# Vision tower on one core: output projections in the first three steps of the feed-forward loop, rare experts first, output bias added behind the features, class rows on another semaphore

## The chip, the cores and the metric

One of the eight cores of a Trainium2 chip runs the whole program. The metric is the device time in microseconds (us) of one execution; lower is better. All arithmetic is float32, but for a few one-hot products in bfloat16.

## What is computed

A small vision tower over 32 images. Each image becomes 25 patches, a class row is put in front, and so there are 32 x 26 = 832 rows of 256 numbers. Cut to what matters:

```python
h = patches @ W                                  # 768 -> 256, and the class row in front of each image
h = h + attn0(norm(h)) @ Wo.T + bo               # linear attention ACROSS images, per position; elu(q)+1, elu(k)+1
h = h + ffn0(norm(h))                            # fixed split of the rows over 8 experts:
                                                 #   x + norm(x) @ attn_w.T, gelu(x @ w1[e]), @ w2[e], @ next_w, gelu
h = h + attn1(norm(h))                           # causal linear attention in each image, 16 heads
x = norm(h); s = shared_down(silu(x@sg) * (x@su))        # 256 -> 512 -> 256 for every row
e = argmax(x @ gate_w); x = x * sigmoid(max(x @ gate_w)) # one of 32 routed experts for every row
h = h + s + down[e](silu(x @ gate[e]) * (x @ up[e]))     # 256 -> 512 -> 256, 1.5 MB of weights each
```

With the reference's own inputs 18 of the 32 routed experts get rows. Counted in strips of 32 rows they need: expert 0 three, 3 one, 4 six, 6 five, 8 one, 10 two, 27 two, and 11, 12, 13, 14, 15, 18, 19, 20, 24, 26, 29 one each; 31 strips in all. Among the first 104 rows (group 0) there are rows for 15 experts; four of them have fewer than four rows there: 8 (3 rows), 15 (2), 20 (1) and 26 (2). These are counts of the inputs, not times.

## The kernel before

The 832 rows lie in 8 groups of 104 (four images each). `h` holds them, rows on the partitions. Every stage runs over the groups, and `lagged(steps, stages)` (line 237) writes the order of a software pipeline: in step t it issues, for each `(stage, lag)` in the list, `stage(t - lag)`. The same list idea is written out once for each engine, so each engine has its own fixed order, and semaphores join them.

**Start.** SyncE (SP) issues all loads in one queue (lines 275 to 303). TensorE's `tok(g)` (line 376) makes the patch product of a group, VectorE (DVE) adds the class rows (line 1033), takes the moments, GpSimd (POOL) raises the variance to the power -1/2 (`power`, line 1439, 104x2 elements), DVE normalises, TensorE transposes (`trA`). The second half of `tok(0)` waits until both the second half of the patch weights and the class rows are there (line 383); the identity comes behind the second part of the patches (line 283).

**First attention.** `unit(n)` (line 402), n = 0 to 7, makes the query and key features in eight pieces; ScalarE (ACT) makes relu and exp (lines 809 and 811), DVE `feature_max` (line 1050) and `feature_sum` (line 1056), then TensorE makes the values in seven tiles (line 427), and DVE adds their bias in `v0_evac` (line 1045). Tiles 2 to 6 wait for the evacuation of an earlier one. DVE's order is `feature_sum(n-1)`, `feature_max(n)`, and at the end `v0_evac(0)`, `feature_sum(7)`, `v0_evac(1)` and on. POOL adds the output bias `bo` to the whole of `h` in one instruction (line 1445), as soon as the last group is normalised. Then come the attention products and `wo(g)` (line 459), the output projection of a group; DVE adds it to `h` in `h1_norms(g)` (line 1076).

**Feed-forward loop.** `wo(0)` to `wo(2)` run ahead; then TensorE's loop (line 570) has in step t: `tr1(t-1)` (transpose of the normalised group), `tr2(t-3)`, `nx(t-2)` (the `next_w` product), `xa(t-1)` (the `attn_w` product), `wo(t)` for t of 3 to 7, `up(t-1)` and, three groups behind, `qk1(t-3)` and `v1(t-3)` (projections of the second attention), `down(t-1)`. In the step of group g, ACT makes the eight gelus (line 848) between `up(g)` and `down(g)`; DVE's `xa_evac(g)` (line 1096) lies between `xa(g)` and `up(g)`, its `eo_evac(g)` (line 1103) between `down(g)` and `nx(g)`. `h1_norms(t)` has lag 0 on DVE.

**Second attention.** DVE and TensorE step through the groups; `first_look` (line 1220) reads the routing of group 0 while the rest is still computed, so that SP can load the weights of eight experts early (`early_at`, line 315): the first eight, by index, that group 0 uses. `seen` marks which experts group 0 uses, `seen_rank` is its running sum.

**Shared expert and routing tables.** TensorE makes `shared_up(n)` (line 637), DVE the products `hidden(n)` (line 1256), and between them DVE builds the tables (lines 1264 to 1326): which rows go to which slot, the order of the experts, where their weights lie. An expert's place in the order (its rank) is: the eight early ones by index, then all others by index (`chosen` has one row of 32 flags for each of these two kinds; the tables are running sums over both).

**Routed experts.** Four strips of 32 rows make a quad; the 31 strips are 8 quads, q = 0 to 7, of which TensorE computes gate and up (`strips`, line 698, for both the line 703), then transposes `hw` (`ht`, line 709) and makes the down product of the quad before (line 716). The weights of a quad are copied from one of eight slots (1.5 MB each) to fixed lanes, by DVE (`copy_gate`, `copy_up`, `copy_down`, lines 1334 to 1346) and ACT (line 920), one quad ahead. SP loads the other ten experts with `feed` (line 330), two in flight, n-th into the slot of the expert of rank n; a feed waits until the last quad that uses that slot's expert has been copied (lines 332, 333), and `loaded` is counted by SP in the same queue. While the routed quads run, TensorE also makes the shared down products of groups 2 to 7: by the list `SHARED_AT` one in q = 3, two in q = 4 and three in q = 5. The rows of `h` go out by a DMA of POOL (line 1467), and when all eight are stored, POOL adds the routed rows to the output, one indirect DMA for each quad (line 1460).

## Time and profile before

| | us |
|---|---|
| median of 3 runs | 328.4 |
| lowest and highest of them | 328.25, 331.58 |
| the profiled execution, its own time | 330.19 |
| span of its instructions | 328.3 |
| so, around the span | 1.89 |
| mean granted TensorE clock | 0.984 of full speed |

A profile shows one execution. TensorE's rows are PE (matrix products) and PEld (weight loads); a float32 product of 128x256 or so stands as two records. "Chain" is the chain of waits that ended last, in order of time; in the timeline a row's bracket says how long the engine was idle before it and what ended that. A granted clock of 1.00 is 2.4 GHz, one of 0.50 is 1.2 GHz.

### The profile page before, as it was taken

How to read it: one execution, taken by the hardware profiler on the slowest of the kernel's cores; microseconds unless marked ns; L12 is line 12 of the kernel's file. 1: busy time of each engine (PE TensorE's matmuls, PEld its weight loads, DVE VectorE, ACT ScalarE, POOL GpSimd, SP SyncE). 2: the span in 40 equal slices, each digit the busy share in tenths (PEclk: the TensorE clock that was granted, in tenths of full speed). 3: DMA queues.
4: the chain of work that ended last, by engine and by line, in shares of the span. 5: the costliest groups of instructions: out<-in, count | busy, mean ns of one | idle time of the engine just before them, and what ended most of it. 6: DMA issues, size and time to landing. Idle time of an engine off the chain costs nothing.

```text
span 328.3 us, 6678 instructions
## 1 busy us (share of the span) xinstructions
PE 296.7 (90%) x2495; PEld 213.1 (65%) x2495; DVE 197.9 (60%) x565; ACT 142.5 (43%) x320; POOL 58.4 (18%) x65
## 2 busy tenths in 40 slices
PE   7999969689899999999999898988998999998585
PEld 5776548588799999999887566654454334553131
DVE  0556972413364464554368999848872998727636
ACT  1113555322332242232554756529155876506533
POOL 0124300000010010100000010110741002111853
PEclk9999999879999999999999999999999999999899
DMA  7999998006255170000000000699955658999551
GB/s 255 410 436 417 421 347 216 0 0 216 76 224 184 74 257 2 0 2 0 3 0 3 2 2 2 258 426 431 419 181 186 285 186 310 342 384 388 77 60 21
DMA packets 12906, 61.57 MB, mean 188 GB/s; under 512 B 1562, under 2 KB 7530, under 8 KB 9290
## 3 DMA queue, kind: packets, MB, share of 16 engines
q1 hardware_dynamic: 10890, 58.25, 46.5%
q0 software_dynamic: 1984, 2.89, 4.5%
q8 instruction: 20, 0.33, 0.4%
q14 instruction: 12, 0.10, 0.1%
HBM read 55.09 MB, written 6.04 MB: 186 GB/s over the span
## 4 chain that ended last, share of the span: by engine, by line
PE 60%; DVE 19%; DMA 12%; issue 4%; ACT 3%; POOL 1%; SPq 1%; ACTq 0%; DVEq 0%; POOLq 0%
DMA arena<-experts_dram 10%; PE P L493 10%; PE P L505 9%; PE P L372 9%; PE P L703 5%; PE P L384 5%; PE P L645 4%; PE P L550 4%; DVE cols L1056 2%; PE P L716 2%; PE P L481 2%; PE P L588 2%; DMA arena<-cls_dram 2%; DVE arena L1050 1%; DVE arena L1103 1%
## 5 line engine op out<-in xcount | busy, mean ns | idle before, releaser
L1439 POOL TENSOR_TENSOR rstd<-var,mhalf 104x2 f32<-104x2 f32 x32 | 22.1, 692 | 190.3 <-DVE var L1013 150.5
L372 PE MATMUL P<-arena 128*104 128x256 f32 x192 | 48.4, 386 | 2.2 <-DVE arena L1103 0.8
L703 PE MATMUL P<-arena,cols 128*32 128x512 f32 x288 | 34.7, 622 | 6.3 <-ACT cols L945 5.3
L920 ACT ACTIVATE arena<-arena 128x1024 f32 x31 | 31.6, 1051 | 16.3 <-SPq L351 7.8
L372 PEld LDWEIGHTS P<-arena 128*104 128x104 f32 x192 | 30.1, 170 | 10.8 <-DVE arena L1103 3.0
L493 PE MATMUL P<-arena 128*128 128x104 f32 x256 | 32.7, 290 | 1.6 <-issue 1.0
L493 PEld LDWEIGHTS P<-arena 128*128 128x128 f32 x256 | 32.3, 206 | 2.5 <-issue 2.1
L505 PE MATMUL P<-arena 128*128 128x104 f32 x256 | 29.9, 275 | 2.4 <-ACT arena L848 2.4
L505 PEld LDWEIGHTS P<-arena 128*128 128x128 f32 x256 | 29.7, 192 | 3.1 <-issue 1.4
L848 ACT ACTIVATE arena<-P,arena 128x104 f32<-128x104 f32 x64 | 17.0, 348 | 28.9 <-PE P L493 28.9
L703 PEld LDWEIGHTS P<-arena,cols 128*32 128x32 f32 x288 | 8.7, 113 | 26.3 <-issue 16.8
L645 PE MATMUL P<-cols,arena 128*128 128x416 f32 x64 | 23.8, 520 | 1.8 <-DVE arena L1256 1.8
L833 ACT ACTIVATE arena<-P,arena 128x104 f32<-128x104 f32 x16 | 6.1, 433 | 40.9 <-PE P L472 40.9
L384 PE MATMUL P<-arena 128*104 128x256 f32 x96 | 22.6, 385 | 0.8 <-DMA arena<-cls_dram 0.8
L1103 DVE TENSOR_SCALAR arena<-P,arena 128x104 f32<-128x104 f32 x16 | 4.5, 321 | 25.9 <-PE P L505 25.9
L384 PEld LDWEIGHTS P<-arena 128*104 128x104 f32 x96 | 15.8, 173 | 5.8 <-DMA arena<-cls_dram 1.2
L645 PEld LDWEIGHTS P<-cols,arena 128*128 128x128 f32 x64 | 11.7, 190 | 10.9 <-issue 8.1
L716 PE MATMUL P<-arena,cols 128*32 128x256 f32 x192 | 15.4, 381 | 1.1 <-ACT cols L948 1.1
L550 PE MATMUL P<-arena 128*128 128x104 f32 x128 | 15.7, 275 | 0.0
L550 PEld LDWEIGHTS P<-arena 128*128 128x128 f32 x128 | 15.0, 192 | 0.2
L798 ACT ACTIVATE cols<-P 128x104 f32<-128x104 f32 x16 | 4.3, 366 | 24.2 <-PE P L394 24.2
L1019 DVE TENSOR_SCALAR arena<-h,mv,rstd 104x256 f32<-104x256 f32 x16 | 6.6, 414 | 13.0 <-POOL rstd L1439 13.0
(219 smaller groups left out, 516.5 us busy)
## 6 DMA issues: line engine op xcount, KB each, us to landing
arena<-experts_dram SPq DMA_DIRECT2D x18, 1536.0 KB, 9.6
arena<-experts_dram SPq DMA_DIRECT2D x8, 2048.0 KB, 12.8
sorted_x<-arena SPq DMA_DIRECT2D x1, 2184.5 KB, 38.4
arena<-shared_dram SPq DMA_DIRECT2D x1, 1536.0 KB, 32.7
arena<-patches_dram SPq DMA_DIRECT2D x2, 624.0 KB, 7.4
arena<-w_dram SPq DMA_DIRECT2D x1, 1024.0 KB, 10.5
out_dram<-arena SPq DMA_DIRECT2D x1, 1024.0 KB, 35.8
arena<-patches_dram SPq DMA_DIRECT2D x1, 936.0 KB, 7.8
```

Source lines behind the costliest of these rows:

```text
L372: last = mm(P[b][0:a.shape[1], col:col + D], a, rhs(c), start=(c == 0), stop=(c == chunks - 1))
L384: last = mm(P[g % 2][0:GT, 0:D], pat[:, g, c * GT:(c + 1) * GT], tokw_s[:, c, :], start=(c == 0), stop=(c == FC - 1))
L493: last = mm(bank(3 + m // 4, 4, GT)[:, m % 4, :], w[:, c, m * 128:(m + 1) * 128], xaT[:, c, :], start=(c == 0), stop=(c == DC - 1))
L505: last = mm(P[5][:, m * GT:(m + 1) * GT], w[:, c, m * 128:(m + 1) * 128], fhT[:, c, :], start=(c == 0), stop=(c == HC - 1))
L550: last = mm(bank(6, 4, GT)[:, 2 * w + m, :], w1_s[:, w, c, m * 128:(m + 1) * 128], x2T[:, c, :], start=(c == 0), stop=(c == DC - 1))
L645: last = mm(bank(b, HALF), w[:, c, m * 128:(m + 1) * 128], x3T[:, c, half * HALF:(half + 1) * HALF], start=(c == 0), stop=(c == DC - 1))
L703: last = mm(P[b][part, :], xT[:, c, part], weights(u)[:, c * INNER:(c + 1) * INNER], start=(c == 0), stop=(c == DC - 1), tile_position=(0, ...
L716: last = mm(P[3][part, 0:D], hT[:, c * 128 + STRIP * u:c * 128 + STRIP * (u + 1)], down_of(u, parity)[:, c * D:(c + 1) * D], start=(c == 0 ...
L848: A(fhT[:, m, :], bank(3 + m // 4, 4, GT)[:, m % 4, :], ACT.Gelu, bias=bcol_s[:, B1 + HC * g + m:B1 + HC * g + m + 1])\
L920: return A(to, third(where, n), ACT.Copy)
L1103: last = V.tensor_scalar(eoT[:, c, :], P[5][:, c * GT:(c + 1) * GT], bcol_s[:, B2 + DC * g + c:B2 + DC * g + c + 1], None, ALU.add)
L1439: nc.gpsimd.tensor_tensor(rstd[:, :], var[:, :], mhalf[:, :], ALU.pow).then_inc(s["rstd_ready"], 1)
```

## The change

Four things are changed at once. (1) All eight `wo` run in steps 0 to 2, four of them before the loop's first step, into banks 0, 7, 6 in turn. `xa` stands first in the step, `tr1(t)` just ahead of `down(t-1)`, and DVE normalises group t+1 in step t. (2) The experts that group 0 uses with fewer than four rows come first in the order, then its other experts, then the rest; the tables get three kinds, 96 columns in place of 64. (3) POOL's addition of `bo` waits for the eighth `feature_sum`. (4) The class rows and the identity count on one semaphore, and both are issued ahead of the second part of the patches; the second half of the patch weights has one of its own. The diff, cut:

```diff
+FEW = STRIP // GROUPS            # 4
+KINDS = 3 * EXPERTS              # 96
 def wo_bank(g):
-    return {1: 7, 2: 6}[g] if g in (1, 2) else 0
+    return (0, 7, 6)[g % 3]
 # SP
 if i == 0:
-    sp.dma_start(tokw_s[:, FC // 2:FC, :], tokw[:, FC // 2:FC, :]).then_inc(s["cls_in"], 16)
-    sp.dma_start(clsbuf, cls).then_inc(s["cls_in"], 16)
-if i == 1:
+    sp.dma_start(tokw_s[:, FC // 2:FC, :], tokw[:, FC // 2:FC, :]).then_inc(s["tokw2_in"], 16)
+    sp.dma_start(clsbuf, cls).then_inc(s["ident_in"], 16)
     sp.dma_start(ident[:, :], ident_in).then_inc(s["ident_in"], 16)
 # TensorE
 if g == 0 and c == FC // 2:
-    pe.wait_ge(s["cls_in"], 32)
+    pe.wait_ge(s["tokw2_in"], 16)
 def wo(g):
     if g >= 3:
-        pe.wait_ge(s["x2T_ready"], g - 2)
-        pe.wait_ge(s["h0_ready"], GROUPS + (g if g > 3 else 1))
+        pe.wait_ge(s["h0_ready"], GROUPS + g - 2)
...
-for g in range(3):
+for g in range(4):
     wo(g)
+tr1(0)
+wo(4)
 pe.wait_ge(s["wx_in"], 16)
+xa(0)
+wo(5)
...
+def last_wo(g):
+    if g in (1, 2):
+        wo(g + 5)
-lagged(GROUPS + 3, [(tr1, 1), (tr2, 3), (nx, 2), (xa, 1), (later_wo, 0), (up, 1), (but_last(qk1), 3), (but_last(v1), 3), (down, 1)])
+lagged(GROUPS + 3, [(but_first(xa), 1), (tr2, 3), (nx, 2), (up, 1), (but_last(qk1), 3), (but_last(v1), 3), (but_first(tr1), 0), (last_wo, 0), (down, 1)])
 # VectorE
-dve.wait_ge(s["cls_in"], 32)
+dve.wait_ge(s["ident_in"], 32)
...
 def h1_norms(g):     # h1_add(g), the addition of wo(g) to h, is a function of its own now
...
+    if g < 3:
+        h1_add((1, 3, 4)[g])
     dve.wait_ge(s["rstd_ready"], norms[0])
...
+    if g == 0:
+        h1_add(2)
+    if g == 2:
+        h1_add(5)
+h1_add(0)
+h1_norms(0)
-lagged(GROUPS + 2, [(nx_evac, 2), (xa_evac, 1), (h2_norm, 2), (h1_norms, 0), (but_last(z_evac), 3), (but_last(v_evac), 3), (attention_front, 1),
-                    (eo_evac, 1), (h2_bias, 2)])
+lagged(GROUPS + 2, [(xa_evac, 1), (nx_evac, 2), (h2_norm, 2), (h1_norms, -1), (but_last(z_evac), 3), (but_last(v_evac), 3), (attention_front, 1),
+                    (last_adds, 0), (eo_evac, 1), (h2_bias, 2)])
...
 if g == LOOK + 1:
-    V.tensor_scalar(seen, P[5][:, 256:256 + EXPERTS], 0.0, None, ALU.is_gt)
+    V.tensor_scalar(seen[:, EXPERTS:], P[5][:, 256:256 + EXPERTS], float(FEW), None, ALU.is_ge)
+    V.tensor_scalar(seen[:, 0:EXPERTS], P[5][:, 256:256 + EXPERTS], 0.0, None, ALU.is_gt).then_inc(s["seen"], 1)
...
-    link(V.tensor_tensor_scan(seen_rank, seen, zeros64[:, 0:EXPERTS], 0.0, ALU.add, ALU.add))
-    link(V.tensor_scalar(scratch32, seen_rank, at_k, None, ALU.is_le))
-    link(V.tensor_reduce(own[:, 0:1], scratch32, AX.X, ALU.add))
-    V.tensor_scalar_min(tcol[:, 2:3], own[:, 0:1], float(EXPERTS - 1)).then_inc(s["look"], 1)
+    dve.wait_ge(s["seen"], 1)
+    link(V.tensor_tensor(seen[:, 0:EXPERTS], seen[:, 0:EXPERTS], seen[:, EXPERTS:], ALU.subtract))
+    link(V.tensor_tensor_scan(seen_rank, seen, zeros[:, 0:2 * EXPERTS], 0.0, ALU.add, ALU.add))
+    link(V.tensor_scalar(seen_below, seen_rank, at_k, None, ALU.is_le))
+    link(V.tensor_reduce(own[:, 0:1], seen_below, AX.X, ALU.add))
+    link(V.tensor_scalar_min(own[:, 0:1], own[:, 0:1], float(2 * EXPERTS - 1)))
+    link(V.tensor_scalar(own[:, 1:2], own[:, 0:1], float(EXPERTS), float(-EXPERTS), ALU.is_ge, ALU.mult))
+    V.tensor_tensor(tcol[:, 2:3], own[:, 0:1], own[:, 1:2], ALU.add).then_inc(s["look"], 1)
...
-link(V.tensor_tensor(first_of, scratch64[:, 0:EXPERTS], scratch64[:, EXPERTS:], ALU.add))
+link(V.tensor_reduce(first_of, scratch.rearrange("p (a e) -> p e a", a=3), AX.X, ALU.add))
 # POOL
 pool.wait_ge(s["n_ready"], GROUPS)
+pool.wait_ge(s["qk0_ready"], 8)
 nc.gpsimd.tensor_tensor(h[:, :, :], h[:, :, :], brow_s[0:GT, BO0, :]...to_broadcast([GT, GROUPS, D]), ALU.add)
```

The waits of `tr2`, `qk1(0)` and `v1(0)` on the additions to `h` are set to the new order (`v1(0)` waits for all eight, since bank 7 takes `wo(1)`, `wo(4)` and `wo(7)`). The other table instructions have the same form over 96 columns.

## Rows read from the trace of the kernel before

**Rows 1.** The page's chain that ended last, shares by engine.

```profile
PE 60%; DVE 19%; DMA 12%; issue 4%; ACT 3%; POOL 1%; SPq 1%; ACTq 0%; DVEq 0%; POOLq 0%
```

**Rows 2.** Timeline, TensorE's first wait: start us, us, engine, line, operation.

```profile
7.51 4.20 PE L384 MATMUL P<-arena 128*104 128x256 f32 x18 [0.76 <-DMA arena<-cls_dram]
```

**Rows 3.** Timeline, the bias addition on POOL, DVE beside it, TensorE behind.

```profile
31.55 4.53 POOL L1445 TENSOR_TENSOR h<-h,arena 104x2048 f32<-104x2048 f32 x1 [0.59 <-DVE arena L1019]
32.07 4.45 DVE L1056 TENSOR_TENSOR cols<-arena 128x416 f32<-128x416 f32 x1
...
37.19 0.59 DVE L1056 TENSOR_TENSOR cols<-arena 128x416 f32<-128x416 f32 x1
...
45.03 4.73 PE L372 MATMUL P<-arena,cols 128*128 128x256 f32 x20 [2.81 <-DVE vrow L1045]
```

**Rows 4.** Timeline, DVE additions of PSUM and SBUF with POOL idle, then busy.

```profile
180.41 1.09 DVE L1195 TENSOR_TENSOR arena<-P,arena 104x416 f32<-104x416 f32 x2 [0.83 <-PE P L588]
...
189.73 0.69 POOL L1439 TENSOR_TENSOR rstd<-var,mhalf 104x2 f32<-104x2 f32 x1 [4.34 <-DVE var L1013]
...
190.14 1.09 DVE L1195 TENSOR_TENSOR arena<-P,arena 104x416 f32<-104x416 f32 x2
```

**Rows 5.** Windows: stretch, length, busy us of PE PEld DVE ACT POOL, clock, DMA.

```profile
42.00:44.00 2.00, 0.21 (x1) 0.00 (x0) 1.79 (x5) 1.87 (x4) 0.00 (x0) 1.00 0.94 380
...
64.00:66.00 2.00, 1.44 (x7) 1.28 (x7) 1.53 (x6) 0.56 (x1) 0.06 (x1) 0.50 0.00 0
```

**Rows 6.** Timeline, the first transpose of the loop, behind `wo(2)`.

```profile
61.43 0.55 PE L472 MATMUL P<-ident,arena 104*128 104x104 f32 x4 [1.36 <-DVE arena L1089]
```

**Rows 7.** The chain in order of time, the loop's first two steps.

```profile
64.75 6.52 PE P L493 x32
...
72.41 3.83 PE P L505 x32
...
84.41 3.80 PE P L505 x32
```

**Rows 8.** The chain, one later step, the next one's start, and the last step's gap.

```profile
101.49 0.57 DVE arena L1103 x2
...
104.08 0.86 PE P L372 x4
104.95 3.55 PE P L493 x32
...
114.74 0.57 DVE arena L1103 x2
...
157.10 0.52 issue
```

**Rows 9.** Timeline, DVE's running sums over 32 and 64 columns.

```profile
200.33 0.16 DVE L1227 TENSOR_TENSOR_SCAN arena<-arena 128x32 f32<-128x32 f32 x1
...
226.61 0.29 DVE L1271 TENSOR_TENSOR_SCAN arena<-arena 128x64 f32<-128x64 f32 x1
```

**Rows 10.** Timeline, TensorE's wait behind the tables.

```profile
229.51 3.06 PE L645 MATMUL P<-cols,arena 128*128 128x416 f32 x8 [1.58 <-DVE arena L1256]
```

**Rows 11.** Timeline of SP's queue, all ten feeds in one row.

```profile
250.75 46.27 SPq L334 DMA_DIRECT2D arena<-experts_dram  x10
```

**Rows 12.** The chain, first and last of four feeds in a row.

```profile
271.55 7.30 DMA arena<-experts_dram
...
296.68 9.87 DMA arena<-experts_dram
```

**Rows 13.** Timeline, gate and up products of quads 6 and 7.

```profile
298.85 3.64 PE L703 MATMUL P<-arena,cols 128*32 128x512 f32 x32 [1.09 <-ACT cols L945]
...
309.02 5.34 PE L703 MATMUL P<-arena,cols 128*32 128x512 f32 x32 [3.70 <-ACT cols L945]
```

**Rows 14.** Timeline, POOL's row additions, the first and the third.

```profile
302.98 1.71 POOL L1460 DMA_INDIRECT out_dram<-vrow,target x1 [6.37 <-DMA out_dram<-h]
...
306.90 2.01 POOL L1460 DMA_INDIRECT out_dram<-vrow,target x1 [0.30 <-issue]
```

More of the change, by code:

```diff
@@ L176, in tower @@
         slot_i = sb("slot_i", [GT, GROUPS], I32)
-        ranks = flat7[:, 0:640].rearrange("p (a e) -> p a e", a=10)
-        chosen, visits, load, ends, scratch64, zeros64 = (ranks[:, i, :] for i in range(6))
-        strips_of, raw = ranks[:, 6, 0:EXPERTS], ranks[:, 6, EXPERTS:]
-        others, seen = ranks[:, 7, 0:EXPERTS], ranks[:, 7, EXPERTS:]
-        seen_rank, scratch32 = ranks[:, 8, 0:EXPERTS], ranks[:, 8, EXPERTS:]
-        first_lg, first_max = ranks[0:GT, 9, 0:EXPERTS], ranks[0:GT, 9, EXPERTS:EXPERTS + 1]
-        first_of = scratch32
+        ranks = flat7[:, 0:10 * KINDS].rearrange("p (a e) -> p a e", a=10)
+        chosen, visits, load, ends, scratch, zeros = (ranks[:, i, :] for i in range(6))
+        strips_of, raw, others = (ranks[:, 6, i * EXPERTS:(i + 1) * EXPERTS] for i in range(3))
+        scratch32, first_of = ranks[:, 7, 0:EXPERTS], ranks[:, 7, EXPERTS:2 * EXPERTS]
+        first_lg, first_max = ranks[0:GT, 8, 0:EXPERTS], ranks[0:GT, 8, EXPERTS:EXPERTS + 1]
+        seen, seen_rank, seen_below = chosen[:, 0:2 * EXPERTS], visits[:, 0:2 * EXPERTS], scratch[:, 0:2 * EXPERTS]
         early_at = sb("early_at", [1, EARLY], I32)
@@ L656, in _ @@
             v1(GROUPS - 1)
-            def but_first(stage):
-                return lambda g: g > 0 and stage(g)
             lagged(GROUPS + 4, [(av, 1), (logits, 4), (tr3, 3), (but_first(den), 0), (but_first(scores), 0), (wo1, 1), (spread, 0), (shared_first, 2)])
@@ L1262, in _ @@
             rank, first, slot = (lgm[:, i * GROUPS:(i + 1) * GROUPS] for i in (3, 4, 5))
-            two = "p (a e) -> p a e"
+            kinds = "p (a e) -> p a e"
             V.tensor_scalar(raw, P[5][:, 256:256 + EXPERTS], 1.0 / STRIP, (STRIP - 1) / (2.0 * STRIP), ALU.mult, ALU.add)
-            V.scalar_tensor_tensor(chosen[:, EXPERTS:], P[5][:, 256:256 + EXPERTS], 0.0, others, ALU.is_gt, ALU.mult)
+            V.scalar_tensor_tensor(chosen[:, 2 * EXPERTS:], P[5][:, 256:256 + EXPERTS], 0.0, others, ALU.is_gt, ALU.mult)
             link(V.tensor_tensor(big[:, :, :], P[4][0:GT, 0:256].rearrange("p (g e) -> p g e", e=EXPERTS), onehot_b[:, :, :], ALU.mult))
@@ L1305, in _ @@
             some, rounds = tfl[:, 0:FEEDS], tfl[:, FEEDS:FEEDS + 1]
-            link(V.tensor_scalar(some, bcol_s[0:1, C_FEED:C_FEED + FEEDS], visits[0:1, EXPERTS - 1:EXPERTS], None, ALU.add))
-            link(V.tensor_scalar(some, some, visits[0:1, 2 * EXPERTS - 1:2 * EXPERTS], None, ALU.is_lt))
+            link(V.tensor_scalar(some, bcol_s[0:1, C_FEED:C_FEED + FEEDS], hits[0:1, :], None, ALU.add))
+            link(V.tensor_scalar(some, some, total[0:1, :], None, ALU.is_lt))
             link(V.tensor_reduce(rounds, some, AX.X, ALU.add))
             V.tensor_scalar(table[:, T_FEEDS:T_FEEDS + 1], rounds, 1.0, None, ALU.max)
-            link(V.scalar_tensor_tensor(scratch64, ends, at_k, chosen, ALU.is_le, ALU.mult))
+            link(V.scalar_tensor_tensor(scratch, ends, at_k, chosen, ALU.is_le, ALU.mult))
             V.tensor_scalar_add(own[:, 1:2], total, -1.0)
@@ L1314, in _ @@
             hidden(3)
-            link(V.tensor_reduce(own[:, 0:1], scratch64, AX.X, ALU.add))
+            link(V.tensor_reduce(own[:, 0:1], scratch, AX.X, ALU.add))
             link(V.tensor_scalar(own[:, 0:1], own[:, 0:1], own[:, 1:2], None, ALU.min))
@@ L1321, in _ @@
             all_quads, loops = tfl[:, FEEDS + 1:FEEDS + 1 + MAX_QUADS], tfl[:, FEEDS + 1 + MAX_QUADS:]
[L1322 removed]
+            link(V.tensor_scalar(all_quads, bcol_s[0:1, C_QUAD:C_QUAD + MAX_QUADS], ends[0:1, KINDS - 1:KINDS], None, ALU.is_lt))
             link(V.tensor_reduce(loops, all_quads, AX.X, ALU.add))
```

54 lines of the change are left out of this document (29 added, 25 removed).

## The prediction

> **What bounds the kernel now.** I read the page's chain first, then the chain in order of time, then the timeline where the chain changes its engine, and the windows for the clock. The chain lies 60% on TensorE, 19% on DVE and 12% on DMAs [rows 1]: TensorE is the bound, with a few stretches where something else is. They are these.
>
> Features, 31 to 45 us: POOL adds the output bias for 4.53 us. A `feature_sum` that DVE begins half a microsecond later takes 4.45 us; the same operation takes 0.59 us with POOL idle [rows 3]. From there DVE is late until the values, where TensorE stands still for 2.81 us [rows 3].
>
> Start of the loop, 57 to 88 us: TensorE waits for the first normalisation (1.36 us ahead of `tr1`) [rows 6], runs at half clock from about 64 us [rows 5], so that `up(0)` takes 6.52 us where a later `up` takes 3.55 [rows 7, 8], and waits for the last gelus (71.27 to 72.41, 1.14 us) [rows 7].
>
> Steady loop: one step is 114.74 - 101.49 = 13.25 us, 0.86 of it `wo` [rows 8], and the rest nearly all products. The last full step has a gap of 0.52 us where no `wo` is left between `xa` and `up` [rows 8].
>
> Routed experts, 250 us on: the ten feeds are issued from 250.75 to about 297 us, though nothing but their slots holds them back [rows 11], and at the end the chain is four feeds one behind the other, 7.30 to 9.87 us each, until 306.55 [rows 12]. But that chain overstates what they cost: TensorE meanwhile has the shared down products, and its real waits are 1.09 us ahead of quad 6 and 3.70 ahead of quad 7 [rows 13]. Behind the longer one the gate and up products take 5.34 us in place of 3.64 [rows 13].
>
> **The change, part by part.** All terms are for the profiled execution: 328.3 us of span and 1.89 around it, 330.19; the median of the runs is 1.8 lower, 328.4. I take the sum from either.
>
> *Class rows.* `tok(0)` waited 0.76 us for the class rows, the last of two transfers of one semaphore [rows 2]. They are the smallest thing in the queue there; without them I estimate 0.2 us less, and the identity, now ahead of the second patches, takes about as much back for `tok(1)`. Between -0.2 and 0.76 us; value 0.2.
>
> *Bias addition.* `feature_sum(0)` ends 3.9 us earlier (4.45 - 0.59) [rows 3]. What is late next is TensorE itself: units and two value tiles fill it until 42.2, and that is where its wait of 2.81 us began [rows 3], so the gain is 2.8 and not 3.9. POOL now adds from about 42.8 to 47.3 us, and its result is wanted only when the first `wo` is added to `h`, ahead of the normalisation that `tr1(0)` at 61.43 - 2.8 = 58.6 waits for [rows 6]: some eight microseconds of cover. Nothing else is queued on POOL before that. Beside it DVE has `v0_evac` and the mask products, one operand in PSUM and one in SBUF. Such additions take 1.09 us for two whether POOL is idle or begins 0.41 us before them [rows 4], while the operation that was held has both operands in SBUF [rows 3]. So I take no hold; the other end is the rest of the addition, 4.5 us.
>
> *Start of the loop.* `wo(3)` comes right behind `wo(2)`; `wo(4)` fits between `tr1(0)` and `xa(0)`, `wo(5)` between `xa(0)` and `up(0)`. These were waits, so `up(0)` begins as before against what lies ahead, and DVE's extra additions (0.42 us each or less) fall into the wait for POOL's power or behind the normalisation; `xa_evac(0)` now queues behind the normalisation of group 1 and is ready at about the same time. TensorE has then hardly half a microsecond of rest after 60 us, where it had 1.36 us and more before it fell to 1.2 GHz [rows 5, 6]. It kept 2.4 GHz through its 2.81 us wait at 42 us [rows 3, 5], so I expect the clock to stay: `up(0)` takes some 3.7 and not 6.52 [rows 7, 8]: gain 2.8. Neither end is shown: 0 if it falls anyway.
> Steps 1 and 2: the gelu waits (1.14 us each) [rows 7] now hold `tr1` (0.55) [rows 6] and `wo(6)`, `wo(7)` (0.86) [rows 8]; `xa` covers the wait for `eoT`. From the start of `down(0)` to that of `down(1)` it was 84.41 - 72.41 = 12.00 us [rows 7]; now `down` 3.8 [rows 7], `nx` and `xa` 2.0 without their wait (102.06 to 104.08), `up` 3.55 [rows 8], `tr1` and `wo` 1.4, less what overlaps at each seam: some 10.5. Gain 1.5.
>
> *Steady steps.* In five steps (t = 3 to 7) `wo` goes, 0.86 us [rows 8], and with `xa` and `tr2` (a microsecond together) between `down` and `nx`, DVE's 0.57 us of `eo_evac` [rows 8] is covered for good; today two transposes cover all but about 0.1 of it. So 1.0 a step, 5.0 together. What `wo` hid, DVE's `xa_evac` between `xa` and `up`, is now hidden by `tr2` and `nx`. It queues on DVE behind `eo_evac` and `h2_bias`; I estimate it ready 1.5 us after `down` ends, from three operations of 0.4 to 0.6, while `up` starts 2.1 to 2.3 after it. ACT's evacuation of `tr1` runs beside `down`, which lasts over 3.5 us. In t = 8 the gap of 0.52 goes [rows 8], the 0.1 too, and `tr1` has left this step: 1.2 less. Bounds: 0.3 a step if most of it comes back as waits, 1.1 at most.
>
> *Look and tables.* DVE is the bound through the second attention (the chain and the timeline show it nearly without a gap from 175 to 213 us). The look chain gets three more linked operations, and four of them work on 64 columns where it was 32: a running sum goes from 0.16 to 0.29 [rows 9]; the three short ones I put at 0.25 each with their wait, and a second comparison at 0.1, as short operations on DVE lie between the two sums of these rows: +1.1 us. In the tables the operations on 96 columns for 64 add, by the same rise of 0.13 us for 32 columns of a running sum and less for the others, 0.3 us ahead of `hidden(1)`, for which TensorE waited 1.58 us already [rows 10], and 0.3 later on: +0.6. Together 1.7 lost, between 0.8 and 2.3.
>
> *Rare experts first.* The order was 0, 3, 4, 6, 8, 10, 12, 13; it becomes 8, 15, 20, 26, 0, 3, 4, 6. In the first order the early eight hold 20 strips, and their slots come free after quads 0, 0, 2, 3, 3, 4, 4, 4; in the new one after quads 0, 0, 0, 0, 1, 1, 3, 4. The number of quads stays 8. (Both lists follow from the strips of each expert and `feed`'s waits.) Pairs of feeds take 7.3 to 9.9 us [rows 12]. At some 8.7 us a pair, feeds 0 and 1 go at 250.75 [rows 11] as now, 2 and 3 at about 260, 4 and 5 at 268.5, 6 at 277 and 7 behind it, landed at 286.5. The last pair waits for quad 5's copy, about 288 (today's third feed of the chain is issued then), and lands at 297. Quad 6 needs feeds 4 to 7 copied while quad 5 runs (from about 290), quad 7 the last pair from about 301: both are there. So 1.09 + 3.70 us of waiting go, and with them the 1.2 GHz behind the second [rows 13], 5.34 - 3.64 = 1.70: 6.5 us. What is late next is TensorE itself: from quad 6 to quad 7 it was 10.17 us, less 3.70 of waiting 6.47 [rows 13], and DVE and ACT copy a quad's weights beside it. Bounds: 0 if the feeds are not what quads 6 and 7 wait for, 6.5 above.
> Quad 0 now needs four early loads and not two, but they are asked for 33 us before it is copied.
>
> Sum: 0.2 + 2.8 + 2.8 + 1.5 + 5.0 + 1.2 + 6.5 - 1.7 = 18.3 us. 330.19 - 18.3 = 311.9 for the profiled execution, 328.4 - 18.3 = 310.1, say **310.0 us** for the median.
>
> **The rivals.**
> *POOL's row additions take the end over.* They start when the eight stores have landed, 302.98, and follow at 1.96 us ((306.90 - 302.98) / 2) [rows 14]. With the quads 6.5 us earlier the eighth is wanted by 316. If the stores land no sooner, the eighth is issued at 302.98 + 7 x 1.96 + 0.5 for the wait between = 317.2, and with additions slowed by denser copies (below) 2 us later: the tail gives 4 us and not 6.5: 312.5. For it: the stores are 0.1 MB each and cross the same feeds. Against: the last feeds now end 9 us earlier. DVE's copies beside an addition make it 2.01 us and not 1.71 [rows 14], so denser copies cost 0.3 each, 2 us more at worst.
> The Trainium skill, SBUF — State Buffer, SBUF: two separate sides, says more: copies of DVE from SBUF to SBUF lock out the writing of descriptors for POOL's DMAs, about 620 ns alone against 3100. By that each of seven additions beside copies would cost 2.5 us more, an estimate of 17 us that would eat the whole gain. The rows with and without copies differ by 0.3 us, so the trace does not bear this out at that size; I give it 0.01 of what is unnamed below.
>
> *The clock falls at the loop's start all the same:* 2.8 us less gain, 312.8. For it, that TensorE waits in three places there today; against, that the new products fill them.
>
> *The hold moves on to the values.* If POOL's addition holds `v0_evac` as it held `feature_sum`, TensorE waits some 4.5 us in the value tiles: the 2.8 turn into a loss of 1.7, 314.5. Against it stand rows 4.
>
> *The order of experts changes nothing* (the look sees other counts, or quads 6 and 7 wait for something else): 310.0 + 6.5 = 316.5.
>
> *The other side: slower.* The new step is a ring of waits: `tr1(t)` just ahead of `down`, ACT behind the gelus, `xa`, DVE's `xa_evac` behind `eo_evac` and `h2_bias` and DVE's normalisation of the next group ahead of the evacuations of `qk1` and `v1`, with POOL's power in it. If one of these isn't beside products but behind them, each of the eight steps pays it. The slack on `up` is 0.6 us. The change is slower only from 18.3 / 8 = 2.3 us of new wait a step. What stands in series at the loop's start today, from `tr1` to `up` (61.43 to 64.75, 3.3 us) [rows 6, 7], is the price where it lies open in each step: 310.0 + 8 x 3.3 = 336.
>
> **How the numbers follow.** The forecast 0.62; row additions 0.12; clock 0.07; hold 0.07; order without effect 0.06; ring of waits 0.03, and 0.03 for something unnamed that leaves it near the old time. A measurement of this kernel tells about 1% from no change, 3.3 us. All cases but the last two are faster by over 1%: 0.95; same 0.03, slower 0.02. The range reaches up over the first three rivals, and two of them together, to 316; down to 306, where the waits that go at the loop's start bring a little more than their terms, and the bounds of the tables and class rows are at their best.
>
> **What would show it.** `feature_sum(0)` at 0.6 us and no long DVE row beside POOL's 4.5 us; no wait of TensorE in the values; granted clock 1.00 from 60 to 72 us, `up(0)` under 4; steps of 12.2 to 12.3 us between the evacuations of line 1103's kind; feeds issued from 251 to 288 and none on the chain; the gate products of quads 6 and 7 at 3.64 us each without a wait before them. The prediction is wrong if steps stay above 12.8, if feeds stay on the chain, or if the last rows are POOL's additions in one unbroken run.

## The result, and the profile after

| us | before | after |
|---|---|---|
| median, lowest, highest (4 runs each, taken side by side) | 329.69, 328.25, 331.58 | 311.12, 310.22, 312.54 |
| the profiled execution, its span | 330.19, 328.3 | 310.22, 308.3 |
| mean granted clock of the profiled execution | 0.984 | 0.999 |

The ratio of the times is 0.944, 95% interval 0.937 to 0.951. The forecast was 310.0 us, 306 to 316: 18.4 us under the 328.4 it started from. Measured are 18.6 us under the 329.69 of the runs beside it.

The start of the profiled execution, timeline of TensorE, after:

```profile
6.95 1.54 PE L384 MATMUL P<-arena 128*104 128x256 f32 x6 [0.34 <-DMA arena<-tokw_dram]
8.93 2.84 PE L384 MATMUL P<-arena 128*104 128x256 f32 x12 [0.43 <-DMA arena<-patches_dram]
...
39.96 6.61 PE L372 MATMUL P<-arena,cols 128*128 128x256 f32 x28
...
58.16 0.58 PE L471 MATMUL P<-ident,arena 104*128 104x104 f32 x4 [0.41 <-DVE arena L1098]
...
61.50 3.71 PE L492 MATMUL P<-arena 128*128 128x104 f32 x32
```

The wait for the class rows [rows 2] is gone; shorter ones for weights and patches stand in its place. The values are one row of 28 records with no wait in it, where there were 2.81 us [rows 3]. The first transpose waits 0.41 us and not 1.36 [rows 6], and `up(0)` takes 3.71 us and not 6.52 [rows 7]. Beside the values, DVE and POOL, same view:

```profile
31.76 0.59 DVE L1061 TENSOR_TENSOR cols<-arena 128x416 f32<-128x416 f32 x1
...
42.45 4.53 POOL L1470 TENSOR_TENSOR h<-h,arena 104x2048 f32<-104x2048 f32 x1 [11.80 <-DVE cols L1061]
...
43.01 0.43 DVE L1050 TENSOR_TENSOR vrow<-P,arena 128x256 f32<-128x256 f32 x1 [0.39 <-PE P L372]
```

`feature_sum(0)` is at 0.59 us, and the `v0_evac` beside POOL's addition takes 0.43: no hold. The two windows of [rows 5] after (columns as there):

```profile
42.00:44.00 2.00, 2.00 (x10) 1.71 (x11) 1.17 (x4) 1.16 (x1) 1.54 (x1) 1.00 0.94 381
...
64.00:66.00 2.00, 2.00 (x18) 1.91 (x18) 0.00 (x0) 1.27 (x7) 0.00 (x0) 1.00 0.00 0
```

The chain in order of time, the loop's start and one later step, after:

```profile
61.66 3.55 PE P L492 x32
...
66.44 3.75 PE P L504 x32
...
76.75 3.79 PE P L504 x32
...
101.11 3.57 PE P L504 x32
...
113.19 3.57 PE P L504 x32
```

A step is 12.08 us (113.19 - 101.11) for 13.25 [rows 8], and between its rows nothing but TensorE stands. The look on DVE and what follows it on TensorE, timelines after:

```profile
185.46 0.13 DVE L1248 TENSOR_TENSOR arena<-arena 128x32 f32<-128x32 f32 x1
185.62 0.29 DVE L1249 TENSOR_TENSOR_SCAN arena<-arena 128x64 f32<-128x64 f32 x1
...
186.87 0.16 DVE L1254 TENSOR_TENSOR tcol<-own 128x1 f32<-128x1 f32 x1
```

```profile
188.09 0.92 PE L610 MATMUL P<-arena 104*32 104x104 f32 x32 [0.95 <-DVE arena L1215]
```

Before, TensorE's row of this kind came 0.1 us behind the one ahead of it (202.24 behind 202.11); now it waits for the addition that stands behind `first_look` on DVE. ("The look" below is this part of DVE's work.) The routed stage after: SP's feeds, the gate products of quads 6 and 7, POOL's stores and row additions (timelines):

```profile
237.05 39.42 SPq L334 DMA_DIRECT2D arena<-experts_dram  x10
```

```profile
283.99 3.64 PE L708 MATMUL P<-arena,cols 128*32 128x512 f32 x32
...
290.38 3.64 PE L708 MATMUL P<-arena,cols 128*32 128x512 f32 x32
```

```profile
278.91 0.55 POOL L1492 DMA_DIRECT2D out_dram<-h  x1 [7.17 <-DVE h L1374]
...
282.37 2.83 POOL L1492 DMA_DIRECT2D out_dram<-h  x1 [1.18 <-DVE h L1374]
287.46 1.74 POOL L1485 DMA_INDIRECT out_dram<-vrow,target  x1 [2.26 <-DMA out_dram<-h]
...
299.79 1.64 POOL L1485 DMA_INDIRECT out_dram<-vrow,target  x1 [0.30 <-issue]
...
301.74 1.72 POOL L1485 DMA_INDIRECT out_dram<-cols,target  x1 [0.25 <-issue]
```

Both quads run without a wait, at 3.64 us [against rows 13]; the feeds are issued over 39.4 us and not 46.3 [rows 11]. The ending chain, by engine:

```profile
PE 78%; DVE 13%; issue 3%; DMA 2%; ACT 2%; POOL 1%; SPq 1%; ACTq 0%; DVEq 0%
```

DMAs fell from 12% to 2% and DVE from 19% to 13% [rows 1]. The starts of the same instructions, before and after, account for the whole 20.0 us of span (all in us; the last two columns are what was gained since the line above):

| stretch, up to the start of | before | after | gained in it | predicted |
|---|---|---|---|---|
| the first `unit` | 28.92 | 28.57 | 0.35 | 0.2 |
| the attention products | 49.75 | 46.57 | 2.83 | 2.8 |
| `up(0)` | 64.75 | 61.66 | -0.09 | 0 |
| `down(0)` | 72.41 | 66.44 | 2.88 | 2.8 |
| `down(1)` | 84.41 | 76.75 | 1.69 | 1.5 |
| `down(6)` (five steps) | 150.91 | 137.34 | 5.91 | 5.0 |
| `down(7)` | 164.06 | 149.05 | 1.44 | 1.2 |
| `shared_up` (the look) | 217.12 | 203.02 | -0.9 | -1.1 |
| the first quad (the tables) | 249.56 | 235.86 | -0.4 | -0.6 |
| quad 6 | 298.85 | 284.06 | 1.1 | 1.1 |
| quad 7 | 309.02 | 290.45 | 3.8 | 3.7 |
| what follows quad 7's gate products | 314.36 | 294.02 | 1.8 | 1.7 |
| the last transposes | 325.64 | 305.61 | -0.3 | 0 |

### The profile page after: what moved, and what is told of

It is laid out like the page before. It is cut to its first block, busy times and chain, and to the rows that moved or that the text cites. A ratio compares the mean times of both kernels' runs of the same rounds, so it can differ in the third digit from the quotient of the medians.

```text
span 308.3 us, 6677 instructions
## 1 busy us (share of the span) xinstructions
PE 289.0 (94%) x2495; PEld 208.4 (68%) x2495; DVE 195.7 (63%) x569; ACT 142.9 (46%) x320; POOL 58.5 (19%) x65
## 4 chain that ended last, share of the span: by engine, by line
PE 78%; DVE 13%; issue 3%; DMA 2%; ACT 2%; POOL 1%; SPq 1%; ACTq 0%; DVEq 0%
PE P L372 12%; PE P L504 9%; PE P L708 9%; PE P L492 9%; PE P L384 6%; PE P L721 5%; PE P L653 5%; PE P L549 4%; PE P L411 4%; PE P L480 2%; DMA arena<-patches_dram 2%; PE P L596 2%; PE P L714 2%; DVE arena L1215 1%; DVE arena L1167 1%
## 5 line engine op out<-in xcount | busy, mean ns | idle before, releaser
L372 PE MATMUL P<-arena 128*104 128x256 f32 x192 | 47.7, 383 | 1.2 <-ACT arena L830 0.5
L708 PE MATMUL P<-arena,cols 128*32 128x512 f32 x288 | 33.0, 596 | 1.8 <-DVE arena L1365 0.6
L492 PEld LDWEIGHTS P<-arena 128*128 128x128 f32 x256 | 29.8, 192 | 0.6
L504 PE MATMUL P<-arena 128*128 128x104 f32 x256 | 30.0, 275 | 0.0
L504 PEld LDWEIGHTS P<-arena 128*128 128x128 f32 x256 | 29.3, 192 | 0.8 <-issue 0.4
L492 PE MATMUL P<-arena 128*128 128x104 f32 x256 | 29.7, 274 | 0.0
L384 PE MATMUL P<-arena 128*104 128x256 f32 x96 | 22.4, 381 | 1.4 <-DMA arena<-patches_dram 1.1
L853 ACT ACTIVATE arena<-P,arena 128x104 f32<-128x104 f32 x64 | 17.0, 348 | 14.2 <-PE P L492 14.2
L1120 DVE TENSOR_SCALAR arena<-P,arena 128x104 f32<-128x104 f32 x16 | 4.5, 321 | 19.7 <-PE P L504 19.7
L1492 POOL DMA_DIRECT2D out_dram<-h x8 | 8.1, 1016 | 46.5 <-DVE h L1374 46.5
L549 PE MATMUL P<-arena 128*128 128x104 f32 x128 | 15.7, 275 | 0.0
L549 PEld LDWEIGHTS P<-arena 128*128 128x128 f32 x128 | 15.0, 192 | 0.2
```

What stands on the lines that cost most here:

```text
L372: last = mm(P[b][0:a.shape[1], col:col + D], a, rhs(c), start=(c == 0), stop=(c == chunks - 1))
L384: last = mm(P[g % 2][0:GT, 0:D], pat[:, g, c * GT:(c + 1) * GT], tokw_s[:, c, :], start=(c == 0), stop=(c == FC - 1))
L492: last = mm(bank(3 + m // 4, 4, GT)[:, m % 4, :], w[:, c, m * 128:(m + 1) * 128], xaT[:, c, :], start=(c == 0), stop=(c == DC - 1))
L504: last = mm(P[5][:, m * GT:(m + 1) * GT], w[:, c, m * 128:(m + 1) * 128], fhT[:, c, :], start=(c == 0), stop=(c == HC - 1))
L549: last = mm(bank(6, 4, GT)[:, 2 * w + m, :], w1_s[:, w, c, m * 128:(m + 1) * 128], x2T[:, c, :], start=(c == 0), stop=(c == DC - 1))
L708: last = mm(P[b][part, :], xT[:, c, part], weights(u)[:, c * INNER:(c + 1) * INNER], start=(c == 0), stop=(c == DC - 1), tile_position=(0, ...
```

## The experiments

The theory: the four parts add up, each by the waits it takes out of TensorE's row. The rivals: that one part (the three projections) carries the rest; that the clock at the loop's start falls for another reason than TensorE's waits; that the feeds had lost their weight; and that POOL's row additions end the kernel now. Twelve kernels ran in three groups, each with its own runs of the kernel before: medians 330.26, 329.47 and 329.38.

**One part at a time.** Only (3), one line:

```diff
 pool.wait_ge(s["n_ready"], GROUPS)
+pool.wait_ge(s["qk0_ready"], 8)
```

> The kernel before with one line more: POOL's bias addition waits for the eighth feature_sum. If the hold of DVE is what the 2.8 us were: the long feature_sum shrinks from 4.45 to 0.59 us, the wait of TensorE in the values goes, and the time falls by 2.8 us (ratio 0.991). If the hold only moves on to the value evacuations behind it, one of them takes over 4 us and the time stays or rises by up to 1.7 us.

Measured: 325.63 us, ratio 0.987 (0.981 to 0.994), so 4.2 us and not 2.8. Its profile has the values as one row without a wait, as after, and from the first `unit` to the attention products it is 18.00 us for 20.83: 2.83, which is the term. Its interval (about 2.2 us to either side) takes in 2.8 as well as 4.2; two places where more may come from show in the next run and in this profile's `up(0)`, which takes 5.42 us and not 6.50. At the loop's start, where the waits still are, the clock still falls (window of e1):

```profile
62.00:64.00 2.00, 2.00 (x11) 2.00 (x11) 1.13 (x6) 0.00 (x0) 0.69 (x1) 0.50 0.00 0
```

Only (2), the order of experts and the wider tables:

```diff
+FEW = STRIP // GROUPS
+KINDS = 3 * EXPERTS
...
+    link(V.tensor_tensor(seen[:, 0:EXPERTS], seen[:, 0:EXPERTS], seen[:, EXPERTS:], ALU.subtract))
```

> The kernel before with the new order of the experts and its wider tables alone. If quads 6 and 7 wait for the feeds and the parts add up: 6.5 us gained behind the tables, 1.3 lost in the look and the tables, 5.2 together (ratio 0.984). If the tail is bound by POOL's row additions or by something else than the feeds: less than 3 us gained there, and a net of 0 to 1.5 us.

Measured: 326.65 us, ratio 0.989 (0.982 to 0.996): 3.5 us. Quads 6 and 7 have no wait here either (gate products at 300.46 and 306.85, 3.64 us each). In the profiled run, what is missing lies in the values, which this part doesn't touch (timeline of TensorE and a window behind its wait, e2):

```profile
45.05 6.29 PE L373 MATMUL P<-arena,cols 128*128 128x256 f32 x20 [2.83 <-DVE vrow L1046]
```

```profile
46.00:48.00 2.00, 2.00 (x6) 1.58 (x5) 0.42 (x1) 0.00 (x0) 0.00 (x0) 0.50 1.11 294
```

The same wait and the same 20 records as in [rows 3], but at 1.2 GHz: 6.29 us and not 4.73, 1.6 us lost. That closes the profile (3.5 us of span and 1.6 make 5.1 for 5.2). It does not explain the medians, for how many of the other runs of before lost it there too is not known. The profiled run of before had kept the clock there; the runs of e3, e6, e7 and e12, which have this wait too, lost it (6.42 us each).

Only (1), the projections:

> The kernel before with the projections in steps 0 to 2, the new places of xa and tr1 and DVE's new order, and nothing else. If the loop's terms stand by themselves: 2.9 at the start (clock), 1.7 in step 2, 5.9 in steps 3 to 7 and 1.4 in step 8, 11.9 us together (ratio 0.964). If the clock at the loop's start owes something to the earlier bias change (TensorE's 2.8 us wait in the values), it falls here as before and only some 9 us are gained.

Measured: 317.32 us, ratio 0.963 (0.956 to 0.970): 12.2 us, as expected. `up(0)` takes 3.71 us. Its ending is not TensorE's: POOL's additions run unbroken from 294.83, six microseconds behind the end of the last store's issue, and they end the chain.

All four, run beside these three:

> The changed kernel itself, as the measure for the three beside it on the same chip: ratio 0.944, 18.5 to 20 us less than the kernel before. If the parts add up, the gains of the three single parts and 0.3 us for the class rows make this number within 1 us.

Measured: 310.33 us (310.13 to 310.63), ratio 0.940 (0.934 to 0.947), 19.7 us. The three alone give 4.2 + 3.5 + 12.2 = 19.9. No part carries another: each is worth something alone. But each gain is known to about 2 us only, so that the sum closes to 0.2 is in part luck. In the profiled runs the three make 5.8 + 3.5 + 12.7 = 22.0 us of span for 19.5. Of the 12.7 of e3, 10.0 are there by `down(7)` (154.03 for 164.06), 4.2 more come at quads 6 and 7, which wait 2.32 us together where they waited 4.79, and of which the last stays at 3.64 us; POOL's end gives 1.5 back. The quads of e1 wait less too (3.43 us), and a wait for feeds can be taken out only once.

Only (4), the class rows, run once:

> The kernel before with only the class rows and the identity moved onto another semaphore. TensorE's wait of 0.76 us in tok(0) becomes about 0.35 for the weights' second half, the first unit begins 0.3 us earlier (28.92 before), and the whole time is the same within a measurement's spread. Rival, that the identity ahead of the patches gives all of it back: the first unit begins as before.

Measured: 330.05 us. The wait became one of 0.31 us for the weights, and the first `unit` begins at 28.64 for 28.92. But e1, without this edit, has it at 28.64 too, so from this run alone the 0.3 us can't be told from chance.

**Is it the feeds?** After, with the experts in the old order:

```diff
-FEW = STRIP // GROUPS
+FEW = 2 * TOKENS
```

> The kernel after with its experts in the old order (the limit of four rows raised to more than any expert has, so that none of the first kind exists); the tables keep their 96 columns. If the feeds' slots are what quads 6 and 7 waited for, the feeds come back on the chain and the routed stage takes 5 to 6.5 us longer: about 316.5 (309.9 to 311 for the kernel after beside it), with waits of about 1 and 3.7 us ahead of the gate products of quads 6 and 7. Rival, that the faster front moved the bound to POOL's row additions: under 3 us longer.

Measured: 314.98 us (313.44 to 316.69 in three runs; the ratio leaves out a fourth of 319.56 with a clock of 0.977), ratio 0.955 (0.946 to 0.965), 4.7 above the 310.33 of the kernel after, and one of the two waits is back, on TensorE's row (timeline) and on the chain in order of time:

```profile
295.23 5.29 PE L708 MATMUL P<-arena,cols 128*32 128x512 f32 x32 [2.74 <-ACT cols L950]
```

```profile
259.89 6.47 DMA arena<-experts_dram
...
283.61 9.14 DMA arena<-experts_dram
```

Quad 7 waits 2.74 us and quad 6 not at all; with the 1.2 GHz behind it this makes 4.4 us of the 74.2 from the first gate products to the last transposes (69.8 after). So the order is worth 4.4 here and not the 6.6 of the table above: the chain of four feeds takes 32.9 us in place of 35.0 [rows 12]. It is not the faster front alone that does this. In the seven profiled runs with the old order the waits of quads 6 and 7 together are 4.79 (before), 4.32 (e12), 3.43 (e1), 3.15 (e6), 2.97 (e9), 2.74 (e5) and 2.32 us (e3), and quad 7 runs at 1.2 GHz in before, e12, e1 and e5 and at 2.4 in the others. The order is worth 2.3 to 6.5 us, and the profile of before stands at the upper end. The rest of this profile's difference, 2 us, is a clock that fell in the second attention (below). The rival that the feeds had lost their weight is out.

**Is it the waits that drop the clock?** The kernel before with five useless products in TensorE's waits at the loop's start, no order and no wait changed:

```diff
+def fill(n):
+    for _ in range(n):
+        mm(P[3][:, 0:D], zrow[:, 0:128], zrow[:, 0:D], start=True, stop=True)
...
+    fill(2)        # behind wo(2), and behind tr1(0); fill(1) behind xa(0), ahead of up(0)
```

> The kernel before with five useless products of the bank P[3] (a zero row against a zero row, 256 columns, the result never read) put into TensorE's waits at the loop's start: two behind wo(2), two behind tr1(0), one ahead of xa(0). No order and no wait changes. If it is TensorE's rest of over a microsecond there that lets the clock fall, the granted clock stays 1.00 from 60 to 72 us, up(0) takes about 3.6 and not 6.52 us, and the kernel is 2 to 2.8 us faster than the one before. Rival, that the clock falls for another reason (it falls a set while after the values, or the gain came from the three projections themselves): up(0) stays near 6.5 us and the time is the same within 1 us.

Measured: 325.27 us, ratio 0.989 (0.981 to 0.996). The last filler stands behind `xa(0)`, not ahead of it as the expectation says. In its timeline the fillers are `L565`; `up(0)` follows them at full clock, as the window shows:

```profile
61.61 1.03 PE L565 MATMUL P<-arena 128*128 128x256 f32 x4
63.04 0.58 PE L472 MATMUL P<-ident,arena 104*128 104x104 f32 x4 [0.40 <-DVE arena L1103]
...
66.17 3.79 PE L493 MATMUL P<-arena 128*128 128x104 f32 x32
```

```profile
64.00:66.00 2.00, 2.00 (x13) 1.29 (x11) 0.35 (x2) 1.98 (x5) 0.00 (x0) 1.00 0.00 0
```

From the attention products to `down(0)` it was 19.66 us (71.11 - 51.45) for 22.66 (72.41 - 49.75): 3.0 us for work that computes nothing. It was the rest that cost the clock. The median gained 4.2 us, more than that; in this profile the values lost 1.7 us to the clock, and quads 6 and 7 gave 3.3 (3.15 us of wait for 4.79, and 3.64 us for the 5.34 of quad 7), which the fillers did not bring. The same in the values as well, four more products ahead of the third value tile:

```diff
+if i == 2:
+    pe.wait_ge(s["z0_ready"], 3)
+    for _ in range(4):
+        mm(P[6][:, 0:D], zrow[:, 0:128], zrow[:, 0:D], start=True, stop=True)
```

> The kernel before with the five useless products at the loop's start, and four more of the same kind ahead of the third value tile, where TensorE waits 2.8 us for DVE; the waits for data stay as they are. If the clock that fell behind the values in most profiled runs with this wait (6.3 to 6.4 us for 20 records in place of 4.73) fell because of the wait, the values take 4.7 us in every run, the granted clock is 1.00 through 40 to 72 us, and the runs lie together at about 324.3 to 324.8 (those of the run with five products lay at 324.7 and 324.9 with a clock of 1.000 and at 325.7 and 325.9 with 0.995). Rival, that it falls at random and not for the wait: still some runs at 325.7 with a clock of 0.995.

Timeline of TensorE, fillers and the value tiles behind them:

```profile
42.00 1.89 PE L426 MATMUL P<-arena 128*128 128x256 f32 x8
44.99 4.73 PE L372 MATMUL P<-arena,cols 128*128 128x256 f32 x20 [1.10 <-DVE vrow L1063]
```

The profiled run (325.08, clock 0.999) is as the theory had it: 4.73 us. But the median of ten runs is 326.69 (325.08 to 329.89, ratio 0.993, 0.989 to 0.997), with mean clocks down to 0.978, and so no better than the 325.27 with five. In the profiled run POOL's row additions end the chain, unbroken from 302.40, so that this kernel could not give all that TensorE gained. Only one run has a trace, so where the others lost their clock stays open; that the wait is the whole cause in the values is not shown.

**The hold, at another place.** After, with POOL's addition behind the fourth `feature_sum`:

```diff
-pool.wait_ge(s["qk0_ready"], 8)
+pool.wait_ge(s["qk0_ready"], 4)
```

> The kernel after, with POOL's addition of the output bias waiting for the fourth feature_sum in place of the eighth, so that it runs beside the features again, at another place. If a POOL operation of SBUF operands holds the DVE operation that has two operands in SBUF and no other, one feature_sum takes about 4.4 us and not 0.59, and TensorE waits 2 to 3 us in the values: 313 to 315, against about 310.5 of the kernel after. Rival, that the 4.45 us of before came from something else at that moment (the first features, loads still landing): no feature_sum above 1 us, and the time as of the kernel after.

Measured: 315.83 us (315.72 to 317.48), ratio 0.962 (0.955 to 0.969), 5.5 above the kernel after. Timelines of POOL, of DVE beside it and of TensorE behind it:

```profile
36.80 4.53 POOL L1470 TENSOR_TENSOR h<-h,arena 104x2048 f32<-104x2048 f32 x1 [6.10 <-DVE cols L1061]
```

```profile
36.67 0.65 DVE L1055 TENSOR_SCALAR arena<-P,arena 128x416 f32<-128x416 f32 x1
37.43 4.35 DVE L1061 TENSOR_TENSOR cols<-arena 128x416 f32<-128x416 f32 x1
```

```profile
45.24 6.42 PE L372 MATMUL P<-arena,cols 128*128 128x256 f32 x20 [3.33 <-DVE vrow L1050]
```

The `feature_max` beside POOL's first half microsecond (its tensor in PSUM) takes its usual 0.65; the `feature_sum` behind it (both in SBUF) takes 4.35. The hold moves with POOL's instruction, and it prices the hold at this place: 3.3 us of wait and 1.7 of clock (6.42 for 4.73). The Trainium skill, SBUF — State Buffer, Who interferes with whom, has the rule: a DVE instruction with two SBUF inputs contends with a POOL instruction that reads SBUF, one with at most one SBUF input, outside what the page calls the 2-port perf modes, does not. This trace agrees on the first (4.35 us). For the second the `feature_max` is weak evidence, since it had begun 0.13 us before POOL; the `v0_evac` at 43.01 in the kernel after, which began while POOL was adding and took 0.43 us, agrees with it.

**Does POOL end the kernel, and is anything left?** After, with the shared down products at other quads:

```diff
-SHARED_AT = ((), (), (), (2,), (3, 4), (5, 6, 7), (), ())
+SHARED_AT = ((2,), (3,), (4,), (5,), (6,), (7,), (), ())        # e8
+SHARED_AT = ((2,), (), (), (3,), (4, 5), (6, 7), (), ())        # e10
+SHARED_AT = ((2,), (), (3,), (4, 5), (6, 7), (), (), ())        # e11
```

> The kernel after with the six shared down products in quads 0 to 5, one each, in place of one, two and three in quads 3, 4 and 5, since the feeds now need no cover there. If the stores of the rows and POOL's additions behind them are close to the end, earlier shared products give earlier stores and fill the waits of the first two quads: 0.5 to 1.5 us faster than the kernel after, about 309.5. Rival, that TensorE's quads are the bound whatever lies between them: within 0.5 us of the kernel after. Other side: the copies of quads 1 and 2 are not ready earlier, and the feeds are waited for again, up to 2 us slower.

Measured: 313.17 us (311.35 to 313.47). From the first gate product to the eighth it is 53.4 us for 54.5, so TensorE did gain 1.1. The median is 2.8 us above the kernel after all the same. Of the 3.3 us by which this profile's span is longer, 2.1 were lost ahead of the first quad, in a second attention whose clock fell (below), and the rest at the end (timeline of POOL, the last store and the first addition):

```profile
283.01 2.83 POOL L1492 DMA_DIRECT2D out_dram<-h  x1 [4.56 <-DVE h L1374]
290.80 1.74 POOL L1485 DMA_INDIRECT out_dram<-vrow,target  x1 [4.96 <-DMA out_dram<-h]
```

The last store is issued at about the same time as after (282.37), but POOL's wait for its landing is 5.0 us and not 2.3, with a pair of feeds on the way beside it (`280.34 8.52 DMA arena<-experts_dram` on the chain; that it delays the landing was not tested), and POOL's additions then run unbroken to the end and stand on the chain.

> The kernel after with the shared down product of group 2 in quad 0, those of 3, of 4 and 5, and of 6 and 7 in quads 3, 4 and 5. In the run with all six spread out TensorE's quads gained 1.1 us (53.4 us from the first to the eighth gate product, for 54.5), but the last store landed later, beside the last feeds, and POOL's additions ended the kernel. If the store of the last group is early enough here, both gain: 309.2 to 309.5, beside 310.2 of the kernel after at full clock. Rival, that POOL's additions are the bound as soon as TensorE gains anything: 310.2 or more.

Measured: 311.06 us (310.32 to 312.25), ratio 0.944 (0.938 to 0.950): the same as the kernel after. Here TensorE ends the chain, and from the first gate products to the last transposes it is 68.6 us for 69.8; but this profile lost 2.3 us to the clock in the second attention. Whether the 1.1 us is there in the median, four runs can't say.

> As the run before it, but with the products of group 3 in quad 2, of 4 and 5 in quad 3, and of 6 and 7 in quad 4: all stores are issued a quad earlier, so that POOL's additions may begin some 6 us earlier, while the weights of quads 6 and 7 get less cover (two shared down products, 3.5 us, no longer lie behind their copies' feeds). If POOL's additions bind, this one is the faster of the two, about 309; if the feeds do, quads 6 or 7 wait again, 1 to 3 us slower than the run before it.

Measured: 315.16 us (311.39 to 315.75). POOL's additions begin at 278.92, 8.5 us earlier than after, and have time to spare, but the weights of quad 7 are late (timeline of TensorE):

```profile
294.16 5.08 PE L708 MATMUL P<-arena,cols 128*32 128x512 f32 x32 [4.14 <-ACT cols L950]
```

Another 1.0 us of this profile is the clock in the second attention. So the new order still needs some shared products in quad 5 as cover: with none (e11) quad 7 waits 4.14 us, with one (e8) 0.23, with two (e10) not at all. No version here is shown to beat the kernel after.

## Why the prediction was right, and where its sizes were off

The median came out at 311.1 for 310.0, the profiled execution at 310.2 for 311.9. The mechanism of every part was the one forecast. The nearness of the totals has luck in it: the terms of the profiled execution came out 1.7 us too small together (20.0 for 18.3; one by one between 0.3 too large and 0.9 too small), the clock in the second attention took back in some runs what the steady steps gave beyond their term, and the largest term, the feeds, was read from the profile in which they cost most.

*Class rows:* 0.35 for 0.2. One pair of runs can't tell it from chance; over all profiled runs the first `unit` begins at 28.62 on average in the eight with the edit (28.31 to 28.79) and at 28.89 in the six without (28.64 to 29.05), so 0.27 us is the better figure. The wait moved on to the second weights and then the patches.

*Bias:* "the gain is 2.8 and not 3.9", as TensorE itself is late next: 2.83. That DVE's additions from PSUM are not held stands too (0.42 us each beside POOL), so the rival of the hold is out, and e7 shows the price of a hold where it is real. The rows it was argued from were thin: the POOL row of [rows 4] ends 0.28 us into the additions, and could have held them no longer than that. What the step lacked is that the wait sometimes took the clock with it. It said "it kept 2.4 GHz through its 2.81 us wait", from one profile; in five of the six profiled runs with this wait and no filler in it the clock fell behind it, 1.6 to 1.7 us. Part (3) is worth 2.8 or 4.4, and e1 measured 4.2, too coarsely to tell which.

*Start of the loop:* the clock stays at 1.00, gain 2.88 for 2.8; e6 shows that the waits were the cause. The second step gained 1.69 for 1.5.

*Steady steps:* 1.18 us each for 1.0, and 1.44 for 1.2 in t = 8. The mechanism (0.86 of `wo`, and `xa` and `tr2` over DVE's `eo_evac`) is right. The step lost 0.31 us beside `wo` (13.25 - 12.08 - 0.86), where I had 0.1. The 0.1 itself was right: from the end of `down` to `nx` it was 0.64 us on the chain, and the two transposes, now part of the row, take 0.54. What the sum had at nothing is `nx`, chain in order of time, before and after:

```profile
115.36 1.11 PE P L372 x4
```

```profile
105.76 0.87 PE P L372 x4
```

Behind a wait the four records stand as 1.11 us, in an unbroken row as 0.87: 0.24 a step, and the same again in t = 8. Five steps make 0.9 us over the term, the largest miss in the sum. No ring of waits formed.

*Look and tables:* 0.9 and 0.4 for 1.1 and 0.6 in the profiled run, and here the step was incomplete. The delay of the look opens a wait of 0.95 us on TensorE, between two of 0.31 and 0.36 that were there before, and in most runs the clock falls behind it. From the first score products to the last, in every profiled run of this study:

| look | us from first to last start |
|---|---|
| old (before, e1, e3, e6, e9, e12) | 37.3, 37.2, 37.2, 37.3, 37.2, 37.2 |
| new, clock 1.00 throughout (after, e2) | 38.2, 38.1 |
| new, clock fallen (e4, e7, e11, e5, e8, e10) | 38.9, 39.0, 39.1, 40.1, 40.1, 40.5 |

One of these, the second attention of e10, windows, and TensorE's timeline with the wait and a later output projection:

```profile
190.00:192.00 2.00, 1.74 (x12) 1.08 (x12) 1.86 (x9) 0.81 (x3) 0.23 (x1) 0.57 0.03 8
192.00:194.00 2.00, 2.00 (x34) 1.81 (x34) 0.67 (x4) 0.26 (x1) 0.46 (x1) 0.50 0.36 59
```

```profile
188.29 0.92 PE L610 MATMUL P<-arena 104*32 104x104 f32 x32 [0.95 <-DVE arena L1215]
...
193.60 2.03 PE L372 MATMUL P<-arena 128*104 128x256 f32 x4
```

The output projection takes 2.03 us where it takes 1.11. So the look costs 0.9 us in the best run, and 1.6 to 3.3 in six of eight. That the longer look is what brings the fall is read from these fourteen runs; filling that wait was not tried. It fits the runs of the kernel after that lie at 311.7 and 312.5 with clocks of 0.987 and 0.988, beside 310.2 and 310.5 with 0.999 and 0.994, and would explain why the median is above the best profile by 0.9.

*Rare experts first:* 6.6 us for 6.5 in the profiles of before and after, wait by wait: 1.1, 3.8, 1.8. In e5 it was 4.4, and over the seven profiled runs with the old order it would have been 2.3 to 6.5. That the term met its profile so well is luck of the profile. The last feed was issued 39.4 us behind the first, for the 37 of my list (288 - 250.75) and the 46.3 of before.

*The end:* my sum had nothing for it, and 0.3 us were lost. The rival of the row additions was nearer than its chance of 0.12 suggests: after, POOL adds without a break from 287.46 to 303.5, which in the prediction was a sign of being wrong, and the seventh addition ends at 301.43 where the last quad's rows are ready at 300.4. The last addition lands at 305.56 (DVE's row that waited 0.18 us for it begins at 305.74), and the last transposes, which the chain goes through, begin at 305.61. So it held by almost nothing. In e3, e8 and e9 the additions did take the end over.

*The time of the additions* beside denser copies is at most 1.97 us, no more than in [rows 14]; the rule of the Trainium skill that I set aside for them shows elsewhere, in the last section.

## What to carry to other kernels

A wait on TensorE is priced twice, by its length and by the clock it may cost behind it, and one profile doesn't tell which of the two a kernel pays: look at the clock of every run, and compare the same stretch over several profiles. Work that must be done anyway belongs into those waits, and an edit that delays another engine by a microsecond should be checked for the wait that it opens there. Where transfers are held back by slots, order the users of the slots by how soon they finish, before buying more slots or earlier issues; and measure each part of a combined change alone, but compare the profiles stage by stage as well: here the medians closed to 0.2 us, while single parts lay 1 to 2 us off their terms.
